# Two products over chosen experts: four experts of 32 rows to a tile instead of two of 64, on one core of Trainium2

## The reference

```python
def _L0_ffn_ref(x, f_know, r_know, W_fk, b_fk, W_rk, b_rk, emb_fk, emb_rk):
    ...
    NF, NR, R, DS, K = (128, 128, 128, 64, 4)
    def feature_fn(x, neurons, weights):          # neurons f_know: [128, 192, 128]
        all_h = jnp.einsum('bsd,ndr->bsnr', x, neurons)
        return jnp.einsum('bsnr,bsn->bsr', all_h, weights)
    def restore_fn(h, neurons, weights):          # neurons r_know: [128, 128, 192]
        all_out = jnp.einsum('bsr,nrd->bsnd', h, neurons)
        return jnp.einsum('bsnd,bsn->bsd', all_out, weights)
    ...
    w_fk, _ = topk_sparsify(jax.nn.softmax(logits_fk, axis=-1), K)
    w_rk, _ = topk_sparsify(jax.nn.softmax(logits_rk, axis=-1), K)
```

## Time and profile before

| what | us |
|---|---|
| median of 3 runs | 959.34 (957.8 to 959.43) |
| the profiled execution | 960.5 |
| its span in the trace | 958.8 |
| PE busy | 799.6 (83%) |
| DVE busy | 668.5 (70%) |
| POOL busy | 546.1 (57%) |
| ACT busy | 324.2 (34%) |
| mean granted clock of PE | 0.869 of full speed |

### The profile page before, as it was taken

One profiled execution on the slowest core, in us unless ns is written; L12 is line 12 of the kernel. 1 busy time (PEld: TensorE's weight loads), 2 busy tenths in 40 slices (PEclk: granted clock), 3 DMA queues, 4 the chain that ended last, 5 costly groups with the idle time before them and its releaser, 6 DMA issues.

```text
span 958.8 us, 21711 instructions
## 1 busy us (share of the span) xinstructions
PE 799.6 (83%) x6428; PEld 651.6 (68%) x6428; DVE 668.5 (70%) x4100; ACT 324.2 (34%) x887; POOL 546.1 (57%) x758
## 2 busy tenths in 40 slices
PE   5689999999999999999755688999987699499800
PEld 3688888888888777776543467899876358456700
DVE  2199999999989899899899677673443254155433
ACT  0124443443444354454322012233211146434700
POOL 5256665655656656566377266006775677775075
PEclk9779998898998799799765699999997799899955
DMA  9325455345314253441019577556899698499533
GB/s 323 112 88 204 147 204 201 134 180 209 107 57 148 90 163 121 135 129 51 14 60 279 171 258 245 151 145 182 257 410 410 207 325 282 160 302 349 191 97 92
DMA packets 81580, 177.21 MB, mean 185 GB/s; under 512 B 12953, under 2 KB 38233, under 8 KB 78649
## 3 DMA queue, kind: packets, MB, share of 16 engines
q1 hardware_dynamic: 56088, 120.62, 37.7%
q10 hardware_dynamic: 14112, 32.12, 8.9%
q0 software_dynamic: 11264, 23.09, 7.9%
HBM read 94.25 MB, written 81.53 MB: 183 GB/s over the span
## 4 chain that ended last, share of the span: by engine, by line
PE 46%; DVE 29%; POOL 9%; issue 8%; DMA 5%; ACT 1%; SPq 1%; POOLq 0%; DVEq 0%; ACTq 0%
DVE work L1388 9%; DVE top L1382 7%; PE bank L1243 6%; PE bank L1296 5%; PE bank L1298 5%; PE bank L1241 4%; PE bank L1226 4%; PE bank L1282 3%; PE bank L985 3%; POOL early L749 3%; PE bank L1030 3%; PE bank L1005 2%; POOL slots_x L694 2%; DVE s_hit L1501 2%; DMA early<-slots_x 2%
## 5 line engine op out<-in xcount | busy, mean ns | idle before, releaser
L1388 DVE MATCH_REPLACE8 work<-top,work 128x68 f32<-128x68 f32 x896 | 179.3, 211 | 0.0
L1382 DVE MAX8 top<-work 128x8 f32<-128x68 f32 x896 | 128.9, 213 | 8.4 <-ACT tru L800 7.6
L1641 DVE COPY place<-bank 96x512 f32<-96x512 f32 x98 | 66.2, 685 | 84.1 <-PE bank L1226 83.6
L749 POOL DMA_INDIRECT early<-slots_h,s_all x68 | 65.0, 956 | 72.7 <-DMA slots_h<-m_y 52.2
L1650 DVE COPY place<-bank 128x256 f32<-128x256 f32 x98 | 40.9, 423 | 91.9 <-PE bank L1282 91.8
L985 PE MATMUL bank<-early,xp 128*128 128x192 f32 x432 | 92.5, 378 | 7.5 <-DMA xp<-in_a_x 5.1
L985 PEld LDWEIGHTS bank<-early,xp 128*128 128x128 f32 x432 | 89.3, 230 | 9.5 <-DMA xp<-in_a_x 5.4
L749 POOL DMA_INDIRECT early<-slots_y,s_all x68 | 65.3, 961 | 52.7 <-DMA slots_y<-m_y 30.5
L694 POOL DMA_INDIRECT slots_x<-early,s_all x68 | 66.4, 976 | 43.6 <-DVE s_all L1514 24.8
L756 POOL DMA_INDIRECT slots_g<-early,s_all x68 | 66.0, 970 | 32.0 <-issue 19.2
L713 POOL TENSOR_TENSOR sc<-work,tru 128x476 f32<-128x476 f32 x32 | 38.0, 1188 | 77.6 <-ACT work L875 77.6
(11 more groups left out here) (186 smaller groups left out, 1741.7 us busy)
## 6 DMA issues: line engine op xcount, KB each, us to landing
early<-slots_x SPq DMA_DIRECT2D x49, 384.0 KB, 3.7
slots_y<-m_y ACTq DMA_DIRECT2D x49, 384.0 KB
slots_h<-m_y ACTq DMA_DIRECT2D x49, 256.0 KB
early<-slots_g SPq DMA_DIRECT2D x49, 256.0 KB, 5.0
f_all<-in_f_know SPq DMA_DIRECT2D x16, 768.0 KB, 5.7
r_all<-in_r_know SPq DMA_DIRECT2D x16, 768.0 KB, 16.2
slots_x<-zero SPq DMA_DIRECT2D x28, 360.0 KB, 3.7
slots_x<-zero SPq DMA_DIRECT2D x28, 336.0 KB, 3.6
```

The source lines that it names most:

```text
L749: nc.gpsimd.indirect_dma_start(g_in[:, i % DEPTH, k, 0:width], None, src, bass.IndirectOffsetOnAxis(s_all[:, r - 1, i, k:k + 1], 0)).then_ ...
L1382: last = nc.vector.max(top8[:, c, :], work[:, par, c, :])
L1388: last = nc.vector.match_replace(work[:, par, c, :], top8[:, c, :], work[:, par, c, :], TAKEN)
L1641: nc.vector.tensor_copy(m_flat[u][0:HALF, :], turn_bank[u][0:HALF, :]).then_inc(sem["m_xt0"], 1)
```

## The change

A tile of 128 slots holds four experts of 32 slots each (`SIZE`, `QUARTERS`), so the experts' own slots are 8 groups a part instead of 16. Spill blocks are 32 rows too: 144 and 128 of them, still 9 and 8 groups. Every matmul of either product now has 32 columns of stationary operand and writes 32 rows of the output tile, in main and spill groups alike; so a spill pair is evicted by one instruction, and no wrong half is computed. In a spill tile, PE takes the matrix of block 0 by a register of its own (one value loaded per tile); the matrices of blocks 1 to 3 are copied beforehand by DVE and ACT, each by its own registers, into a ring of three tiles' buffers (`staged`, `staged_r`), on semaphores `staged_v` and `staged_a`, and `m_used` gives a place back. To make room `m_y` moves into the place of `f_all`. The second product uses four PSUM banks in turn instead of two. Part 1's searches for the first product stand in part 0's main groups, those for the second in part 1's last eight groups; the first sums stand behind groups 3, 5, ... 15 of part 1, the rest behind its end. The piecewise table of tile numbers (`ended`) is built in pieces of 128 places; `iota_t` and some semaphores fall away. The order of main and spill groups stays.

```diff
-SPILLS = tuple((end - first) * P * K4 // HALVED for first, end in PARTS for r in range(2))
+SIZE = 32
+QUARTERS = P // SIZE
+SPILLS = tuple((end - first) * P * K4 // SIZE for first, end in PARTS for r in range(2))
-PART_ROWS = tuple((NE + SPILLS[2 * g]) * HALVED for g in range(2))
+PART_ROWS = tuple((NE + SPILLS[2 * g]) * SIZE for g in range(2))
-PART_MAIN = NE * HALVED // (GROUP * P)
+IN_GROUP = GROUP * P // SIZE
+PART_MAIN = NE // IN_GROUP
+RING = 3
+BY_DVE = ((1, 2), (1,))
+BY_ACT = ((3,), (2, 3))
+FIND_BESIDE = PART_GROUPS[1] - PART_MAIN
+SUM_AT = {3: 0, 5: 1, 7: 2, 9: 3, 11: 4, 13: 5, 15: 6}
...
-        def matrix_numbers(eng, q, jj):
-            at = SPILL_AT[q] + (jj - PART_MAIN) * 2 * GROUP
+        def matrix_numbers(eng, q, tile, quarters):
+            at = SPILL_AT[q] + tile * QUARTERS + quarters[0]
             return nc.values_load_multi_w_load_instructions(
-                tile_e[0:1, at:at + 2 * GROUP], engines=[eng], min_val=0, max_val=NE - 1,
+                tile_e[0:1, at:at + len(quarters)], engines=[eng], min_val=0, max_val=NE - 1,
...
                 for q in range(2 * g, 2 * g + 2):
-                    last = nc.vector.tensor_scalar(ended[:, SPILL_AT[q]:SPILL_AT[q] + SPILLS[q]], iota_t[:, 0:SPILLS[q]], ends[:, q:q + 1], None, ALU.is_ge)
+                    for lo in range(0, SPILLS[q], NE):
+                        n = min(NE, SPILLS[q] - lo)
+                        last = nc.vector.tensor_scalar(ended[:, SPILL_AT[q] + lo:SPILL_AT[q] + lo + n], iota_e[:, 0:n], float(lo), ends[:, q:q + 1], ALU.add, ALU.is_ge)
...
+            def stage_act(r, g, jj, u):
+                if jj < PART_MAIN:
+                    return
+                for t in range(2):
+                    tile = (jj - PART_MAIN) * GROUP + 2 * u + t
+                    at = STAGED_FROM[2 * r + g] + tile
+                    numbers = matrix_numbers(mybir.EngineType.Activation, 2 * g + r, tile, BY_ACT[t])
+                    if at >= RING:
+                        act.wait_ge(sem["m_used"], at - RING + 1)
+                    for e, h in zip(numbers, BY_ACT[t]):
+                        k = at % RING * (QUARTERS - 1) + h - 1
+                        if r == 0:
+                            last = nc.scalar.activation(staged[g][k], in_halves(f_all[0:HALF, bass.ds(e, 1), :].squeeze(1)), ACT.Copy)
+                        else:
+                            last = nc.scalar.activation(staged_r[k], r_all[:, bass.ds(e, 1), :].squeeze(1), ACT.Copy)
+                    last.then_inc(sem["staged_a"], 1)
...
             def keep_first(g, n):
                 for u in range(PAIRS):
                     pair = j * PAIRS + u
+                    made = bank[2 + pair % 4]
+                    if u + 1 < PAIRS:
+                        stage_first(g, n, u + 1)
+                    elif n + 1 < PART_GROUPS[g]:
+                        stage_first(g, n + 1, 0)
                     act.wait_ge(sem["m_mm0"], pair + 1)
-                    if first_order(g)[n] < PART_MAIN:
-                        last = nc.scalar.activation(m_yh[:, d, 2 * u:2 * u + 2, :], made[:, 0:2 * R].rearrange("p (t f) -> p t f", t=2), ACT.Copy)
-                    else:
-                        for h in range(2):
...
+                    nc.scalar.activation(m_yh[:, d, 2 * u:2 * u + 2, :], made[:, 0:2 * R].rearrange("p (t f) -> p t f", t=2), ACT.Copy).then_inc(sem["m_done0"], 1)
...
-            def multiply_first(j, u, pairs, own):
+            def multiply_first(j, u, matrices, at):
                 for t in range(2):
+                    tile = 2 * u + t
+                    if at is not None:
+                        pe.wait_ge(sem["staged_v"], at + tile + 1)
+                        pe.wait_ge(sem["staged_a"], at + tile + 1)
+                    for c in range(2):
+                        for h in (1, 2, 3, 0):
+                            rows = slice(h * SIZE, (h + 1) * SIZE)
+                            last = nc.tensor.matmul(into[rows, t * R:(t + 1) * R], m_xT[u][0:HALF, t, c, rows], matrices[tile][h][:, c, :],
+                                                    start=(c == 0), stop=(c == 1))
+                            if at is not None and c == 1 and h == 3:
+                                last.then_inc(sem["m_used"], 1)
...
+                        for t in range(GROUP):
+                            e = matrix_numbers(mybir.EngineType.PE, 2 * g, spill + t, (0,))[0]
+                            k = (at + t) % RING * (QUARTERS - 1)
+                            matrices.append([in_halves(f_all[0:HALF, bass.ds(e, 1), :].squeeze(1)), *staged[g][k:k + QUARTERS - 1]])
+                        first_product(g, n, matrices, at)
...
+                    for h in (1, 2, 3, 0):
+                        rows = slice(h * SIZE, (h + 1) * SIZE)
+                        last = nc.tensor.matmul(into[rows, t * D:(t + 1) * D], m_hT[u][:, t, rows], matrices[tile][h], start=True, stop=True)
...
-            def turned_first(j):
+            def turned_first(g, n):
                     nc.vector.tensor_copy(m_flat[u][0:HALF, :], turn_bank[u][0:HALF, :]).then_inc(sem["m_xt0"], 1)
+                    stage_dve(0, g, first_order(g)[n], u)
...
-            beside(turned_first, 0, range(2 * (NT - PARTS[0][1])), find_late)
-            beside(turned_first, 1, range(*PARTS[0]), first_sum)
+            dve.wait_ge(sem["sent0"], 16 * K4 * PARTS[0][1])
+            for n in range(PART_GROUPS[0]):
+                turned_first(0, n)
+                if n < FIND_BESIDE:
+                    find_slots(0, PARTS[1][0] + n, 1)
+            for n in range(PART_GROUPS[1]):
+                turned_first(1, n)
+                if n >= PART_GROUPS[1] - FIND_BESIDE:
+                    find_slots(1, PARTS[1][0] + n - (PART_GROUPS[1] - FIND_BESIDE), 1)
+                if n in SUM_AT:
+                    first_sum(SUM_AT[n])
+            for i in range(len(SUM_AT), PARTS[0][1]):
+                first_sum(i)
```

More of the change, by code:

```diff
@@ L59 @@
 PAIRS = GROUP // 2
+RING = 3
+SPILL_GROUPS = tuple(n - PART_MAIN for n in PART_GROUPS)
+STAGED_FROM = tuple((r * sum(SPILL_GROUPS) + g * SPILL_GROUPS[0]) * GROUP for r in range(2) for g in range(2))
+BY_DVE = ((1, 2), (1,))
+BY_ACT = ((3,), (2, 3))
+FIND_BESIDE = PART_GROUPS[1] - PART_MAIN
+SUM_AT = {3: 0, 5: 1, 7: 2, 9: 3, 11: 4, 13: 5, 15: 6}
 LOOK = 2
@@ L1252, in first_product @@
                         turn_first(j + 1, 0)
-                    multiply_first(j, u, pairs, own)
+                    multiply_first(j, u, matrices, at)
             pe.wait_ge(sem["tiles_known"], 2)
@@ L1307, in second_product @@
                         turn_second(j + 1, 0)
[L1308 removed]
+                    multiply_second(j, u, matrices, at)
             pe.wait_ge(sem["m_done0"], GROUPS * PAIRS)
@@ L1632, in form_peaks, with stage_dve @@
                 nc.vector.tensor_tensor(e_all, top[:, :, :, 0:K4], top[:, :, :, 0:1].to_broadcast([P, NT, 2, K4]), ALU.subtract).then_inc(sem["t_weights"], 1)
-            def turned_first(j):
+            def stage_dve(r, g, jj, u):
+                if jj < PART_MAIN:
+                    return
+                if r == 1 and g == 0 and jj == PART_MAIN and u == 0:
+                    for k in range(4):
+                        dve.wait_ge(sem[f"r_in{k}"], 16 * 4)
+                for t in range(2):
+                    tile = (jj - PART_MAIN) * GROUP + 2 * u + t
+                    at = STAGED_FROM[2 * r + g] + tile
+                    numbers = matrix_numbers(mybir.EngineType.DVE, 2 * g + r, tile, BY_DVE[t])
+                    if at >= RING:
+                        dve.wait_ge(sem["m_used"], at - RING + 1)
+                    for e, h in zip(numbers, BY_DVE[t]):
+                        k = at % RING * (QUARTERS - 1) + h - 1
+                        if r == 0:
+                            last = nc.vector.tensor_copy(staged[g][k], in_halves(f_all[0:HALF, bass.ds(e, 1), :].squeeze(1)))
+                        else:
+                            last = nc.vector.tensor_copy(staged_r[k], r_all[:, bass.ds(e, 1), :].squeeze(1))
+                    last.then_inc(sem["staged_v"], 1)
+            def turned_first(g, n):
+                j = FIRST_GROUP[g] + n
                 for u in range(PAIRS):
@@ L1682, in first_sum, with beside @@
                 sum_back(1, i, R)
-            def beside(turned, g, tiles, step, early=0):
+            def beside(turned, g, tiles, step):
                 done = 0
                 for n in range(PART_GROUPS[g]):
-                    turned(FIRST_GROUP[g] + n)
-                    while done < len(tiles) and (done + 1) * (PART_GROUPS[g] - early) <= (n + 1) * len(tiles):
+                    turned(g, n)
+                    while done < len(tiles) and (done + 1) * PART_GROUPS[g] <= (n + 1) * len(tiles):
                         step(tiles[done])
```

159 lines of the change are left out of this document (85 added, 74 removed).

## The result

The changed kernel takes 912.26 us in the median (4 runs, 903.57 to 915.3), the kernel before 958.57 in the same measurement: 0.953 of it, 95% interval 0.943 to 0.963, some 45 us less. Timed again later on one chip it was 912.59 (6 runs) beside 957.15 (11 runs), 0.953 with 0.946 to 0.959. One of these six runs (921.75) was in a slower state, and the median of the other five is 908.37. Its profiled execution took 903.57 with a span of 901.8.

What follows compares the result with a forecast made beforehand. Bound by a chain: part 0's first product, POOL's transfers, part 1's second product, POOL's last fetches. -28.2 + 8.0 - 6.2 - 5.0 + 1 = -30.4 from 960.5 gave 930.1, forecast 929 us against the median; range 906 to 972.

Steps and rivals of the forecast that it cites:

- Quarters four together, and DVE the limit of the main groups: First product, part 0: four column quarters run at once, DVE paces groups at 4.2; main part 35.2 instead of 63.4, -28.2.
- Rival B: Matmuls of a pair: quarters run only two at a time, 1.9 a pair instead of 1.02; total 961; chance 0.08.
- L: Price of a register load of one or two values in spill groups, assumed 0.35 us between bounds 0.073 and 0.87.
- Rival A: Spill groups: loading one value costs as much as eight, 0.87; total 979, or 950 at 0.587; chance above 0.68 us: 0.22.
- The spill groups of the first product at 5.3, +8.0: Part 0: ACT's copies, loads and evictions set each of nine groups at 5.3; 47.7 instead of 39.7 us.
- rival C: Spill groups: ACT's next load hides beside the running copy; groups fall to 4.2 and 4.0; total 906; chance 0.12.
- POOL's waits: POOL's waits for DVE's sums during its indirect transfers: 6 us in place of 12.2, -6.2.
- (b): Link of the bounding chain: POOL's 136 indirect transfers, 1.26 us each, with 12.2 us of waits for sums.
- The second product of part 1: After POOL's transfers: main part 23.5, eight spill groups 41.6 set by ACT; 65.1 instead of 70.1 us, -5.0.
- Part 0's second product at no cost: It runs beside POOL's transfers, 70 us from about 727, done by 797 with 13 to spare; costs nothing.
- (c): Link of the bounding chain: part 1's second product, 70.1 us before, where saved matmul time counts in full.
- Rival D: PE's clock falls in spill groups as PE idles; +18 in the first product, +4 in the second; total 957; chance 0.10.

Runs made afterwards that it cites:

- second profile: The changed kernel unaltered, profiled again when timed later beside the kernel before: 374.7 us from first transposes to end, against 372.8 at first; median 912.59.

## Why the prediction was right, and where it was off

- *Quarters four together, and DVE the limit of the main groups:* right; 34.9 for 35.2, groups 4.1 apart for 4.2. Rival B fell: 1.08 a pair and not 1.9.
- *The price of a load:* L was 0.35, as a mean over loads of one and of two values, and that was too low. PE's loads of one take 0.31 in the middle, but ACT's four of a group show 1.92 in the chain above, 0.48 each; in the changed kernel ACT's loads from 564 to 604 take 0.49 in the mean and those from 808 to 851 0.64. Rival A (0.87 for any load) is out. Of the two pages cited, the trace speaks for the Trainium skill, "Runtime: NRT & Kernel Launch", section "Instruction fetch mechanics" (some 200 ns a register; here 0.21 to 0.23 for each value), except for aligned eights; the 600 ns floor of the Trainium skill, "DMA: Bandwidth & Descriptors", section "Latency and other measured facts", doesn't show, with loads of 0.28.
- *The spill groups of the first product at 5.3, +8.0:* this step failed, by 8 us, over half of the miss of 13 behind the first transposes. I added ACT's loads and copies as if one stood behind the other. The chain without PE's loads shows ACT at 4.5 because a load runs beside the copy before it, which was rival C's mechanism, though not down to its 4.2. Two errors stand against each other in it: copies, evictions, issue and hand-offs, which I had at 3.9, show only 2.6 of the 4.52, and the loads, which I had at 1.4, show 1.9. PE's own 4 L + 3.3 I had at 4.7; it is 4.2, so that both chains set the group. ACT, which I named as the last that PE waits for, is seldom that in the changed kernel: PE stands 8.3 for its own loads and 0.6 for ACT's copies.
- *POOL's waits:* -6.2 forecast; they fell from 12.2 to 1.9, and a transfer cost (173.9 - 1.9) / 135 = 1.27 instead of 1.26, so that (b) is 8.6 shorter. The sum that I had 3 us late, at k = 2, wasn't late, as by my own formula groups of 4.6 have it ready at 38 for 41; the one wait is ahead of the first spread, at 624.2. The part that I gave back to the load of r_all didn't come.
- *The second product of part 1:* -5.0 forecast, -5.7 measured, and that it came so near is in part luck. By its first matmul on a staged matrix its main part takes 25.6 (786.56 to 812.19) for 23.5, its spill groups 38.8 (to 851.0) for 41.6, and the two misses cancel. I had ACT set it, with loads of 0.35 where it has 0.64; PE waits for DVE's copies more, and DVE has output sums between them, which my sum doesn't hold. PE's timeline at the border:
```profile
812.19 0.36 PE L1361 MATMUL bank<-r_more,place 128*32 128x192 f32 x3 [0.45 <-DVE r_more L1724]
```
- *Part 0's second product at no cost:* right, POOL's last spread and a load stand ahead of (c), nothing of PE. *Rival D:* in the first profile the granted clock in part 0's spill groups stayed at 1.00, though PE was busy only 30.7 of 41:
```profile
563.00:604.00 41.00, 30.66 (x645) 23.93 (x646) 25.31 (x72) 23.26 (x69) 9.99 (x10) 1.00 0.53 173
...
808.00:851.00 43.00, 30.77 (x316) 15.74 (x306) 28.74 (x94) 21.86 (x65) 15.61 (x16) 0.72 0.58 194
```
  In the second profile it was 0.92 there, and the spill groups took 41.3 instead of 39.3; so D came for some 8 us and went with 2 us, far from its 18. In the second product's spill groups the clock fell to 0.72 in the first profile. In the second it was 0.88 there:
```profile
811.00:854.00 43.00, 26.62 (x304) 14.04 (x304) 27.65 (x92) 22.05 (x66) 14.68 (x16) 0.88 0.57 185
```
  The stretch to the last slots_y transfer took 70.2 at 0.72 and 70.6 at 0.88, so no cost of the lower clock shows there.

## What to carry to other kernels

When an edit takes a suspected cost away and nothing moves, a second chain of the same length may stand beside it: take both away before calling either free. Count register loads by their values, try eight from a multiple of eight in place of a few, and set them where the engine still has work queued. And compare kernels from the point where their code first differs: here 16 us of spread lay ahead of it.

## What was not expected of the hardware

At the least, a register load takes about 0.07 + 0.21 us for each value on ACT (one 0.28, two 0.49, five 1.11), but eight contiguous values from a multiple of eight take 0.54 to 0.60, less than five, and sixteen 1.10. And 32 matmuls of 32 columns take 1.08 or 1.12 in the two orders that were tried.
